# Values of the windowed attention as whole-width products, the second of each pair on exchanged token blocks

## The chip, the cores and the metric

The kernel runs on one core of a Trainium2 chip. The metric is the device time of one launch in microseconds. The engines: PE (TensorE, matrix products, with weight loads shown as PEld), ACT (ScalarE), DVE (VectorE), POOL (GpSimd) and SP (SyncE, which here issues the DMAs). They run side by side, each its own instruction list in order, and wait for each other through semaphores.

## The reference, cut to what matters

The whole program is four blocks of cross attention and feed-forward on x of 16 x 256 tokens and 128 channels. The change touches one stage, the six layers of windowed self-attention with a feed-forward part (`_L0_ffn_ref`), which takes some 3540 us of the span:

```
x  = shift_tokens(x)                     # channels 64..127 from the token before
q, k, v = split(x @ Wqkv)                # 16 heads of 64
q = l2norm(q) * q_scale;  k = l2norm(k) * k_scale      # then rotary tables with a scale
out = softmax(mask(q @ k_two_windows.T * 8)) @ v_two_windows   # windows of 32 tokens: own and the one before
x = out @ Wo + x
x = ffn_layer(shift_tokens(x)) + x       # layer norm, W1, a * gelu(gate), W2
```

## The kernel before, in words

A layer's 4096 tokens are worked through in 8 passes of 512 tokens (two sequences); 6 layers make 48 passes. A pass has four tiles of 128 tokens, and each tile two groups g of 8 heads, that is four pairs of heads; tile and group together are a chunk. The matrix of V and the output matrix are folded into one, `w_vo`, beforehand, so that "values" are already of 128 output channels per head. For a chunk's group and head n of each pair, the values of a token are 4 x 128 = 512 numbers.

The engines' lists are written out by hand, in `body(p)` of each engine. One round r of a pass projects q and k of tile r (`project_k`, `project_q`), makes the values of tile r's first group and of tile r-1's second group, transposes the rotated q and k of tile r-1 (`turn_q`, `turn_k`), forms its scores, and transposes the probabilities of tile r-2 and mixes its values (`turn_prob`, `mix`). The feed-forward of earlier passes is spread between: `down_proj` and `turn_normed` stand in round 1, the three `gate_proj` in round 2, `up_proj` in rounds 3 and 0. The prediction calls rounds 0 to 3 the first to the fourth. The traces' times below begin with round 1 at 2409.68 us, round 2 at 2428.79, round 3 at 2446.74, round 0 at 2466.47; a pass repeats every 74.43 us.

Values (PE, L825 to L840). `mix` and its window scheme want the two halves of a tile (64 tokens each) side by side: of slot j of `vo`, partitions 64n to 64n+63 hold head n's values of token half j. So `values(t, g, j)` takes the 64 tokens of half j as weights and makes two products of 64 x 512, one for each head of the pairs, into the two partition halves of bank V. `values_a` is half j = 0, `values_b` half j = 1. Both use the one bank V: ACT copies it to `vo` in one instruction of 128 x 512 (`copy_values`, L1290), and PE waits for that copy before it writes the bank again. In PE's list, `values_a` and `values_b` of the second group have project_k, turn_q, turn_prob, project_q and turn_k as neighbours; those of the first group stand between `mix` and `scores`, which work in column strips of 32.

In the trace a float32 product is two records, so the 768 pairs of products at L830 are 3072 records, and one values step of the timeline shows "x4", a whole-width one "x2".

After the copies SP moves the values by 32 partitions to `vo_off` by DMA (`shift_values`, L677), for the windows that begin at odd multiples of 32; `mix` reads `vo` or `vo_off`. `copy_q` (ACT, L1299) brings q to SBUF before `turn_k` may overwrite bank T; `copy_k` (L1304) is already written as two instructions of 64 x 512, one per partition half. `square` (L1283) makes the squares of q and k, after which DVE rotates them (`rotate`, L1036). On POOL, `add_up` and `scale` finish the rotation; `add_up` of the second group is the last of a round, and POOL then waits for the norms.

Of the kernel before, what the change touches and what calls it, by code (L numbers as in the profile page):

```python
# [20 lines left out]
ACT = mybir.ActivationFunctionType  # L21
# [450 lines left out]
def shifted_layers(nc, x_all, ident, ident_bf, dram):  # L472
# [18 lines left out]
    with ExitStack() as ctx:  # L491
# [24 lines left out]
        xs_t = sb("xs_t", [128, 2, SEQ])  # L516
        squares = sb("squares", [128, 2, 2, 512])
# [42 lines left out]
        xs_made = [sem(f"xs_made{s}") for s in range(2)]  # L560
        fold_in, fold_done, fold_made, fold_out = sem("fold_in"), sem("fold_done"), sem("fold_made"), sem("fold_out")
# [48 lines left out]
        def _(sp):  # L610
# [66 lines left out]
            def shift_values(p, t, g):  # L677


                i = 2 * t + g  # L680
                at = 2 * (t % 2)
                sp.wait_ge(vb_copied, count(p, i))
                alone(sp)
                sp.wait_ge(mixed, count(p, i - 4))
                alone(sp)
                for n in range(2):
                    r = 64 * n
                    sp.dma_start(vo_off[r + 32:r + 64, g, at:at + 2, :], vo[r:r + 32, g, at:at + 2, :]).then_inc(vo_moved[g][t % 2], 16)
                    if t % 2:
                        sp.dma_start(vo_off[r:r + 32, g, 2:4, :], vo[r + 32:r + 64, g, 1:3, :]).then_inc(vo_moved[g][t % 2], 16)  # L690
                    else:
                        sp.dma_start(vo_off[r:r + 32, g, 1, :], vo[r + 32:r + 64, g, 0, :]).then_inc(vo_moved[g][t % 2], 16)
# [97 lines left out]
        def _(pe):  # L790
# [17 lines left out]

            def project_k(p, t, g):
# [15 lines left out]
            def values(t, g, j):  # L825


                x = chunk_x(t)[:, 64 * j:64 * j + 64]
                for n in range(2):
                    done = nc.tensor.matmul(bank[V][64 * n:64 * n + 64, :], x, w_vo[:, 4 * g:4 * g + 4, n, :], start=True, stop=True)  # L830
                return done

            def values_a(p, t, g):
                pe.wait_ge(w_vo_in[g], (p + t // PASS_TILES) * 16 + 16)
                pe.wait_ge(vb_copied, count(p, 2 * t + g - 1))
                values(t, g, 0).then_inc(va_done, 1)

            def values_b(p, t, g):
                pe.wait_ge(va_copied, count(p, 2 * t + g))
                values(t, g, 1).then_inc(vb_done, 1)  # L840
# [14 lines left out]
            def scores(p, t, g):  # L855
# [4 lines left out]
                for b in range(4):  # L860
                    for w in range(4):
# [4 lines left out]
                            k_t[:, :, 4 * g + b, at:at + 64],  # L866
# [337 lines left out]
        def _(pool):  # L1204
# [10 lines left out]

            def add_up(p, t, g):
# [20 lines left out]
            def body(p):  # L1237
                for r in range(PASS_TILES):
# [16 lines left out]
                    if on(r):  # L1255
                        add_up(p, r, 1)

# [3 lines left out]
        def _(act):  # L1261
# [28 lines left out]
            def copy_values(p, t, g, j):  # L1290
# [6 lines left out]
                nc.scalar.activation(vo[:, g, 2 * (t % 2) + j, :], flat(V), ACT.Copy).then_inc((va_copied, vb_copied)[j], 1)  # L1297
# [2191 lines left out]
```

## Time and profile before

| | before |
|---|---|
| median of 3 runs | 4854.38 us (4852.14 to 4854.57) |
| profiled execution, its own time | 4843.04 us |
| its span in the profile | 4841.2 us |
| PE busy, share of the span | 4259.6 us, 88% |
| DVE, ACT, POOL busy | 3564.2, 2826.2, 2217.0 us |
| mean granted clock | 0.935 |

Shares of busy time are averages over stages. In the long stretch of the layers each engine's work repeats with every pass, so a timeline of one pass shows all of it. A timeline row is: start in us, duration in us, engine, line, operation, what it writes and reads, how many instructions were merged, and in brackets the idle time before it and what ended that.

### The profile page before, as it was taken

The page shows a single profiled execution, that of the slowest core. Times are in us where ns is not written, and L with a number is a line of the kernel's source. Part 1 is how long each engine was busy: PE and PEld are TensorE (multiplying, and loading weights), DVE is VectorE, ACT ScalarE, POOL GpSimd, SP SyncE. Part 2 cuts the span into 40 slices and gives each one's busy share as a digit, 9 for nine tenths or more (in the row PEclk, how much of TensorE's full clock was granted, in tenths as well). Part 3 has the DMA queues.
Part 4 walks back from the last instruction along what each step waited for, and adds up shares of the span by engine and source line. Part 5 has one row for each costly group of instructions (what it writes and reads, how often), then busy time and mean ns, then how long its engine had stood idle before and what let it go on. Part 6 is the DMA issues. An engine that isn't in the chain of part 4 may idle for free. (4 is left out here: it accounts for less than half of the span.)

```text
span 4841.2 us, 113325 instructions
## 1 busy us (share of the span) xinstructions
PE 4259.6 (88%) x40622; PEld 2404.1 (50%) x40622; DVE 3564.2 (74%) x8488; ACT 2826.2 (58%) x5112; POOL 2217.0 (46%) x1393
## 2 busy tenths in 40 slices
PE   8969999999999999999999999999999964746646
PEld 5645555554555555545555555555555532535534
DVE  6878888887888888878888888788888847456430
ACT  3436666666666666666666666666666635645301
POOL 0006555555555555555555555555555510030015
PEclk9989999999999999999999999999999975868558
DMA  1012222322223222232222322223222210000202
GB/s 40 1 59 65 59 58 55 78 59 56 58 53 77 64 54 59 54 77 62 54 56 60 74 63 54 58 56 74 61 60 54 58 25 1 12 1 6 77 11 30
DMA packets 187686, 245.93 MB, mean 51 GB/s; under 512 B 88661, under 2 KB 129367, under 8 KB 187224
## 3 DMA queue, kind: packets, MB, share of 16 engines
q1 hardware_dynamic: 181912, 239.95, 21.3%
q0 software_dynamic: 5632, 4.33, 0.7%
q8 instruction: 60, 0.98, 0.1%
q14 instruction: 82, 0.67, 0.0%
HBM read 41.13 MB, written 14.30 MB: 11 GB/s over the span
## 5 line engine op out<-in xcount | busy, mean ns | idle before, releaser
L1229 POOL TENSOR_TENSOR f_rot_a<-f_rot_a,f_norm 128x1024 f32<-128x1024 f32 x384 | 731.1, 1904 | 1106.7 <-DVE f_norm L1072 1074.2
L1221 POOL TENSOR_TENSOR f_rot_a<-f_rot_a,f_rot_b 128x1024 f32<-128x1024 f32 x384 | 907.4, 2363 | 353.8 <-issue 298.3
L830 PE MATMUL f_bank<-f_w_vo,f_xs_t 128*64 128x512 f32 x3072 | 828.5, 617 | 9.7 <-ACT f_vo L1297 9.7
L1297 ACT ACTIVATE f_vo<-f_bank 128x512 f32<-128x512 f32 x768 | 457.7, 596 | 579.0 <-PE f_bank L830 572.6
L1288 ACT ACTIVATE f_squares<-f_bank 128x512 f32<-128x512 f32 x768 | 459.1, 598 | 330.2 <-PE f_bank L817 244.5
L1051 DVE TENSOR_TENSOR f_rot_a<-f_bank,f_rot 128x512 f32<-128x512 f32 x768 | 526.8, 686 | 86.3 <-POOL f_rot_a L1221 41.6
L1054 DVE TENSOR_TENSOR f_rot_b<-f_bank,f_rot 128x512 f32<-128x512 f32 x768 | 514.2, 670 | 0.0
L1100 DVE TENSOR_REDUCE f_stat<-f_score 128x8 f32<-128x512 f32 x384 | 262.0, 682 | 280.5 <-ACT f_score L1314 280.5
L1058 DVE TENSOR_REDUCE f_sums<-f_squares 128x16 f32<-128x1024 f32 x384 | 465.1, 1211 | 3.3
L1309 ACT ACTIVATE f_k_t<-f_bank 64x512 f32<-64x512 f32 x768 | 450.4, 586 | 4.8 <-PE f_bank L852 0.3
L817 PE MATMUL f_bank<-f_w_qk,f_xs_t 128*128 128x512 f32 x768 | 431.7, 644 | 7.4 <-ACT f_xs_t L1279 5.9
L887 PEld LDWEIGHTS f_bank<-f_vo_off,f_prob_t 128*32 128x32 f32 x6144 | 309.6, 109 | 242.4 <-issue 242.4
L1235 POOL TENSOR_TENSOR f_prob<-f_score,f_stat 128x512 f32<-128x512 f32 x384 | 401.0, 1044 | 47.0 <-DVE f_stat L1104 47.0
L863 PE MATMUL f_bank<-f_k_t,f_q_t 128*32 128x128 f32 x12288 | 415.0, 276 | 0.0
L887 PE MATMUL f_bank<-f_vo,f_prob_t 128*32 128x128 f32 x6144 | 412.3, 276 | 0.0
L887 PE MATMUL f_bank<-f_vo_off,f_prob_t 128*32 128x128 f32 x6144 | 412.3, 276 | 0.0
L823 PE MATMUL f_bank<-f_w_qk,f_xs_t 128*128 128x512 f32 x768 | 394.0, 595 | 0.4 <-DVE f_rot_b L1054 0.4
L1302 ACT ACTIVATE f_q_t<-f_bank 128x512 f32<-128x512 f32 x384 | 229.0, 596 | 276.6 <-PE f_bank L846 276.6
L863 PEld LDWEIGHTS f_bank<-f_k_t,f_q_t 128*32 128x32 f32 x12288 | 312.0, 109 | 155.4 <-issue 155.4
L1092 DVE TENSOR_REDUCE f_stat<-f_bank 128x8 f32<-128x512 f32 x384 | 262.6, 684 | 132.4 <-PE f_bank L863 131.6
L887 PEld LDWEIGHTS f_bank<-f_vo,f_prob_t 128*32 128x32 f32 x6144 | 309.6, 109 | 0.0
L852 PE MATMUL f_bank<-ident,f_rot_a 128*128 128x128 f32 x1536 | 233.3, 274 | 53.4 <-ACT f_q_t L1302 53.3
(447 smaller groups left out, 7249.8 us busy)
## 6 DMA issues: line engine op xcount, KB each, us to landing
f_vo_off<-f_vo SPq DMA_DIRECT2D x1152, 128.0 KB, 2.3
f_vo_off<-f_vo SPq DMA_DIRECT2D x384, 64.0 KB, 2.0
f_w_qk<-in_Wqk SPq DMA_DIRECT2D x12, 512.0 KB, 5.5
f_vo_dram<-f_vo_pair SPq DMA_DIRECT2D x48, 128.0 KB, 1.8
f_x_shifted<-s_all SPq DMA_DIRECT2D x48, 128.0 KB
f_x_shifted<-s_all SPq DMA_DIRECT2D x48, 127.0 KB
f_w_vo<-f_vo_dram SPq DMA_DIRECT2D x10, 512.0 KB, 4.0
e_w<-in_e_W SPq DMA_DIRECT2D x2, 2048.0 KB
```

The lines of the kernel that those rows point to most:

```text
L817: nc.tensor.matmul(flat(K), chunk_x(t), w_qk[:, 1, 512 * g:512 * g + 512], start=True, stop=True).then_inc(k_done, 1)
L830: done = nc.tensor.matmul(bank[V][64 * n:64 * n + 64, :], x, w_vo[:, 4 * g:4 * g + 4, n, :], start=True, stop=True)
L863: done = nc.tensor.matmul(bank[S][32 * w:32 * w + 32, 128 * b:128 * b + 128], q_t[:, g, 128 * b + 32 * w:128 * b + 32 * w + 32], k_t[:, :, ...
L887: done = nc.tensor.matmul(bank[Y][32 * w:32 * w + 32, 0:128], prob_t[:, g, 128 * b + 32 * w:128 * b + 32 * w + 32], source[:, g, 2 * (t % ...
L1051: nc.vector.tensor_tensor(rot_a[:, slot, n, :].rearrange("p (h d) -> p h d", h=GROUP), source, c_tab, ALU.mult)
L1054: nc.vector.tensor_tensor(rot_b[:, g, n, :].rearrange("p (h s d) -> p h s d", h=GROUP, s=2), swapped, s_tab, ALU.mult).then_inc((q_rotated ...
L1058: nc.vector.tensor_reduce(sums[:, g, :], squares[:, g, :, :].rearrange("p n (h d) -> p (n h) d", h=GROUP), AX_X, ALU.add).then_inc(lengths, 1)
L1221: nc.gpsimd.tensor_tensor(rot_a[:, slot, :, :], rot_a[:, slot, :, :], rot_b[:, g, :, :], ALU.add).then_inc(rot_summed, 1)
L1229: nc.gpsimd.tensor_tensor(heads, heads, over(norm[:, 16 * g:16 * g + 16], [128, 16, HEAD_DIM]), ALU.mult).then_inc(qk_normed, 1)
L1288: nc.scalar.activation(squares[:, g, n, :], flat((Q, K)[n]), ACT.Square).then_inc((q_squared, k_squared)[n], 1)
L1297: nc.scalar.activation(vo[:, g, 2 * (t % 2) + j, :], flat(V), ACT.Copy).then_inc((va_copied, vb_copied)[j], 1)
L1309: done = nc.scalar.activation(k_t[r:r + 64, n, 4 * g:4 * g + 4, at:at + 128], flat(T)[r:r + 64, :].rearrange("p (b n) -> p b n", b=4), ACT ...
```

## The change

The two products of a values step are no longer split by head of the pair on 64 tokens, but one product of all 128 tokens for one head: `values(p, t, g, j)` makes head j of every pair. For j = 1 its weights are the tokens with their two blocks of 64 exchanged (`xs_swap`, made by POOL in `swap_x`, twice a pass, in rounds 1 and 3 behind `add_up`), so that the partition halves fall to the slots that `mix` wants; in slot 1 the heads then stand exchanged. Each bank is copied by two ACT instructions of 64 x 512, whose halves go to different slots. The loads to `vo_off` take the exchanged partitions, and the scores read k of the second window half with its heads exchanged.

```
@@ -514,6 +514,7 @@
         band = sb("band", [128, 2, 512], BF16)
         xw = sb("xw", [128, 2, SEQ])
         xs_t = sb("xs_t", [128, 2, SEQ])
+        xs_swap = sb("xs_swap", [128, 2, 2, 2, 64])
         squares = sb("squares", [128, 2, 2, 512])
         rot_a = sb("rot_a", [128, 4, 2, 512])
         rot_b = sb("rot_b", [128, 2, 2, 512])
@@ -558,6 +559,7 @@
         x_taken = [sem(f"x_taken{s}") for s in range(2)]
         x_turned = [sem(f"x_turned{s}") for s in range(2)]
         xs_made = [sem(f"xs_made{s}") for s in range(2)]
+        xs_swapped = [sem(f"xs_swapped{s}") for s in range(2)]
         fold_in, fold_done, fold_made, fold_out = sem("fold_in"), sem("fold_done"), sem("fold_made"), sem("fold_out")
         vo_moved = [[sem(f"vo_moved{g}{h}") for h in range(2)] for g in range(2)]
 
@@ -687,9 +689,9 @@
                     r = 64 * n
                     sp.dma_start(vo_off[r + 32:r + 64, g, at:at + 2, :], vo[r:r + 32, g, at:at + 2, :]).then_inc(vo_moved[g][t % 2], 16)
                     if t % 2:
-                        sp.dma_start(vo_off[r:r + 32, g, 2:4, :], vo[r + 32:r + 64, g, 1:3, :]).then_inc(vo_moved[g][t % 2], 16)
+                        sp.dma_start(vo_off[r:r + 32, g, 2:4, :], vo[96 - r:128 - r, g, 1:3, :]).then_inc(vo_moved[g][t % 2], 16)
                     else:
-                        sp.dma_start(vo_off[r:r + 32, g, 1, :], vo[r + 32:r + 64, g, 0, :]).then_inc(vo_moved[g][t % 2], 16)
+                        sp.dma_start(vo_off[r:r + 32, g, 1, :], vo[96 - r:128 - r, g, 0, :]).then_inc(vo_moved[g][t % 2], 16)
 
             def shift_x(p, q):
 
@@ -806,6 +808,10 @@
                 t = t % PASS_TILES
                 return xs_t[:, t // 2, 128 * (t % 2):128 * (t % 2) + 128]
 
+            def swapped_x(t):
+                t = t % PASS_TILES
+                return xs_swap[:, t // 2, t % 2, :, :].rearrange("p b n -> p (b n)")
+
             def project_k(p, t, g):
                 i = 2 * t + g
                 pe.wait_ge(w_qk_in[g], p * 16 + 16)
@@ -822,22 +828,22 @@
                 pe.wait_ge(q_rotated, count(p, i - 1))
                 nc.tensor.matmul(flat(Q), chunk_x(t), w_qk[:, 0, 512 * g:512 * g + 512], start=True, stop=True).then_inc(q_done, 1)
 
-            def values(t, g, j):
-
-
-                x = chunk_x(t)[:, 64 * j:64 * j + 64]
-                for n in range(2):
-                    done = nc.tensor.matmul(bank[V][64 * n:64 * n + 64, :], x, w_vo[:, 4 * g:4 * g + 4, n, :], start=True, stop=True)
-                return done
+            def values(p, t, g, j):
+
+                x = chunk_x(t)
+                if j:
+                    pe.wait_ge(xs_swapped[(t % PASS_TILES) // 2], p + t // PASS_TILES + 1)
+                    x = swapped_x(t)
+                return nc.tensor.matmul(flat(V), x, w_vo[:, 4 * g:4 * g + 4, j, :], start=True, stop=True)
 
             def values_a(p, t, g):
                 pe.wait_ge(w_vo_in[g], (p + t // PASS_TILES) * 16 + 16)
                 pe.wait_ge(vb_copied, count(p, 2 * t + g - 1))
-                values(t, g, 0).then_inc(va_done, 1)
+                values(p, t, g, 0).then_inc(va_done, 1)
 
             def values_b(p, t, g):
                 pe.wait_ge(va_copied, count(p, 2 * t + g))
-                values(t, g, 1).then_inc(vb_done, 1)
+                values(p, t, g, 1).then_inc(vb_done, 1)
 
             def turn_q(p, t, g):
                 pe.wait_ge(qk_normed, count(p, 2 * t + g))
@@ -863,7 +869,7 @@
                         done = nc.tensor.matmul(
                             bank[S][32 * w:32 * w + 32, 128 * b:128 * b + 128],
                             q_t[:, g, 128 * b + 32 * w:128 * b + 32 * w + 32],
-                            k_t[:, :, 4 * g + b, at:at + 64],
+                            k_t[:, ::(-1 if w >= 2 else 1), 4 * g + b, at:at + 64],
                             start=False, stop=True, skip_group_check=True)
                 done.then_inc(scores_done, 1)
 
@@ -1213,6 +1219,15 @@
 
             nc.gpsimd.tensor_copy(xw[:, 0, :], x_all[:, 0:SEQ]).then_inc(x_taken[0], 1)
 
+            def swap_x(s, p):
+                pool.wait_ge(xs_made[s], p * 2 + 2)
+                if not isinstance(p, int) or p > 0:
+                    pool.wait_ge(vb_done, count(p, 4 * s - 5))
+                alone(pool)
+                nc.gpsimd.tensor_copy(xs_swap[:, s, :, :, :], xs_t[:, s, :].rearrange("p (t b n) -> p t b n", t=2, b=2)[:, :, ::-1, :]).then_inc(xs_swapped[s], 1)
+
+            swap_x(0, 0)
+
             def add_up(p, t, g):
                 slot = 2 * (t % 2) + g
                 pool.wait_ge(k_rotated, count(p, 2 * t + g))
@@ -1254,6 +1269,10 @@
                         weigh(p, r - 1, 0)
                     if on(r):
                         add_up(p, r, 1)
+                    if r == 1 and has(p, 0):
+                        swap_x(1, p)
+                    if r == 3 and has(p, -1):
+                        swap_x(0, p + 1)
 
             stream(pool, body)
 
@@ -1294,7 +1313,10 @@
 
                     act.wait_ge(mixed, count(p, i - 4))
                     act.wait_ge(vo_moved[g][(t - 1) % 2], moved(p, t - 1))
-                nc.scalar.activation(vo[:, g, 2 * (t % 2) + j, :], flat(V), ACT.Copy).then_inc((va_copied, vb_copied)[j], 1)
+                for half in range(2):
+                    r = 64 * half
+                    done = nc.scalar.activation(vo[r:r + 64, g, 2 * (t % 2) + (half ^ j), :], flat(V)[r:r + 64, :], ACT.Copy)
+                done.then_inc((va_copied, vb_copied)[j], 1)
 
             def copy_q(p, t, g):
                 act.wait_ge(q_turned, count(p, 2 * t + g))
```

In the list of ACT, rounds 2 and 3 of a pass inside the loop, `f_vo` are the values' copies, `f_gate` the gate's copies and gelu, `f_xs_t` the shifted tokens, `f_score` the exponential, `f_q_t` the copy of q. Before:

```order
L1297 ACTIVATE f_vo<-f_bank 128x512
L1334 REGISTER_ALU
L1335 ACTIVATE f_gate<-f_bank,f_cols 85x512
L1340 ACT_TABLE_LOAD
L1340 ACTIVATE f_gate<-f_gate 128x512 x2
L1340 ACTIVATE f_gate<-f_gate 85x512
L1297 ACTIVATE f_vo<-f_bank 128x512
L1285 REGISTER_ALU
L1288 ACTIVATE f_squares<-f_bank 128x512
```

and with the change:

```order
L1318 ACTIVATE f_vo<-f_bank 64x512 x2
L1356 REGISTER_ALU
L1357 ACTIVATE f_gate<-f_bank,f_cols 85x512
L1362 ACT_TABLE_LOAD
L1362 ACTIVATE f_gate<-f_gate 128x512 x2
L1362 ACTIVATE f_gate<-f_gate 85x512
L1318 ACTIVATE f_vo<-f_bank 64x512 x2
L1304 REGISTER_ALU
L1307 ACTIVATE f_squares<-f_bank 128x512
```

Nothing changes place; each copy of the values is two rows in one.

In the list of POOL, rounds 1 and 2 of a pass inside the loop, `f_rot_a<-f_rot_a,f_rot_b` is `add_up`, `f_rot_a<-f_rot_a,f_norm` is `scale`, `f_prob` the weighing. With the change:

```order
L1236 TENSOR_TENSOR f_rot_a<-f_rot_a,f_rot_b 128x1024
L1223 ISA
L1227 COPY f_xs_swap<-f_xs_t 128x256
L1244 TENSOR_TENSOR f_rot_a<-f_rot_a,f_norm 128x1024
L1250 TENSOR_TENSOR f_prob<-f_score,f_stat 128x512
```

The exchange stands between the last `add_up` of round 1 and the first `scale` of round 2, which followed each other before.

## Rows read from the trace of the kernel before

**Rows 1.** Stretch of the layers: engines' busy time (instructions), granted clock, DMA share, GB/s

```profile
core 0: us, PE busy (x) PEld busy (x) DVE busy (x) ACT busy (x) POOL busy (x), PEclk, DMA share, GB/s
700.00:3800.00 3100.00, 2984.03 (x31535) 1595.06 (x31534) 2518.20 (x5368) 2033.08 (x3586) 1785.75 (x1083) 1.00 0.27 61
```

**Rows 2.** PE's timeline in round 1, around the second group's products

```profile
2414.42 0.66 PE L846 MATMUL f_bank<-ident,f_rot_a 128*128 128x128 f32 x4
2414.91 0.60 PE L874 MATMUL f_bank<-ident,f_prob 128*128 128x128 f32 x4
2415.35 1.02 PE L823 MATMUL f_bank<-f_w_qk,f_xs_t 128*128 128x512 f32 x2
2416.21 0.60 PE L852 MATMUL f_bank<-ident,f_rot_a 128*128 128x128 f32 x4
2416.74 1.08 PE L830 MATMUL f_bank<-f_w_vo,f_xs_t 128*64 128x512 f32 x4
2417.75 1.12 PE L817 MATMUL f_bank<-f_w_qk,f_xs_t 128*128 128x512 f32 x2
2418.71 0.38 PE L859 MATMUL f_bank<-f_band,ident_bf 128*128 128x512 bf16 x1
```

**Rows 3.** PE's timeline in round 0, the first group's products and scores

```profile
2405.31 1.08 PE L830 MATMUL f_bank<-f_w_vo,f_xs_t 128*64 128x512 f32 x4
2406.32 0.39 PE L859 MATMUL f_bank<-f_band,ident_bf 128*128 128x512 bf16 x1
...
2407.66 1.08 PE L830 MATMUL f_bank<-f_w_vo,f_xs_t 128*64 128x512 f32 x4
```

**Rows 4.** The costliest groups: busy us, mean ns of one, idle before it

```profile
L1309 ACT ACTIVATE f_k_t<-f_bank 64x512 f32<-64x512 f32 x768 | 450.4, 586 | 4.8 <-PE f_bank L852 0.3
```

**Rows 5.** ACT's timeline in rounds 0 and 1

```profile
2406.44 0.60 ACT L1297 ACTIVATE f_vo<-f_bank 128x512 f32<-128x512 f32 x1 [0.30 <-PE f_bank L830]
...
2415.11 0.60 ACT L1302 ACTIVATE f_q_t<-f_bank 128x512 f32<-128x512 f32 x1
...
2416.90 1.18 ACT L1309 ACTIVATE f_k_t<-f_bank 64x512 f32<-64x512 f32 x2
2418.11 0.60 ACT L1297 ACTIVATE f_vo<-f_bank 128x512 f32<-128x512 f32 x1
2418.91 0.60 ACT L1288 ACTIVATE f_squares<-f_bank 128x512 f32<-128x512 f32 x1 [0.20 <-PE f_bank L817]
```

**Rows 6.** ACT's timeline from the end of round 2 into round 3

```profile
2443.50 0.60 ACT L1297 ACTIVATE f_vo<-f_bank 128x512 f32<-128x512 f32 x1 [0.94 <-PE f_bank L830]
2443.99 0.68 ACT L1335 ACTIVATE f_gate<-f_bank,f_cols 85x512 f32<-85x512 f32 x1
...
2447.56 0.57 ACT L1297 ACTIVATE f_vo<-f_bank 128x512 f32<-128x512 f32 x1
...
2451.25 0.60 ACT L1297 ACTIVATE f_vo<-f_bank 128x512 f32<-128x512 f32 x1
2451.74 0.59 ACT L1302 ACTIVATE f_q_t<-f_bank 128x512 f32<-128x512 f32 x1
```

**Rows 7.** PE's timeline in round 3, the product and turn_k that wait for ACT

```profile
2448.28 1.08 PE L830 MATMUL f_bank<-f_w_vo,f_xs_t 128*64 128x512 f32 x4 [0.20 <-ACT f_vo L1297]
...
2452.39 0.66 PE L852 MATMUL f_bank<-ident,f_rot_a 128*128 128x128 f32 x4 [1.15 <-ACT f_q_t L1302]
```

**Rows 8.** DVE's timeline in round 1, the rotation of k of the second group

```profile
2419.54 0.69 DVE L1051 TENSOR_TENSOR f_rot_a<-f_bank,f_rot 128x512 f32<-128x512 f32 x1
```

**Rows 9.** PE's timeline in round 1, the transposes of the normed tokens

```profile
2422.83 0.66 PE L909 MATMUL f_bank<-ident,f_f_n 128*128 128x128 f32 x4 [0.41 <-DVE s_all L1146]
```

**Rows 10.** POOL's timeline, the first scaling behind round 1's last add_up

```profile
2426.20 1.90 POOL L1229 TENSOR_TENSOR f_rot_a<-f_rot_a,f_norm 128x1024 f32<-128x1024 f32 x1 [5.37 <-DVE f_norm L1072]
```

**Rows 11.** Engines' busy time in two stretches, columns as in rows 1

```profile
2446.00:2456.00 10.00, 8.65 (x63) 3.86 (x51) 7.07 (x16) 9.48 (x17) 7.33 (x5) 1.00 0.20 44
64.90:71.70 6.80, 6.18 (x20) 4.42 (x21) 4.84 (x10) 1.60 (x3) 0.00 (x0) 0.50 0.00 0
```

**Rows 12.** PE's timeline in the cross attention before the layers

```profile
63.36 0.33 PE L215 MATMUL x_bank<-ident,x_xn 128*128 128x128 f32 x1 [2.42 <-DVE x_xn L347]
```

More of the change, by code:

```diff
@@ L560, in shifted_layers @@
         xs_made = [sem(f"xs_made{s}") for s in range(2)]
+        xs_swapped = [sem(f"xs_swapped{s}") for s in range(2)]
         fold_in, fold_done, fold_made, fold_out = sem("fold_in"), sem("fold_done"), sem("fold_made"), sem("fold_out")
@@ L807, in chunk_x, with swapped_x @@
                 return xs_t[:, t // 2, 128 * (t % 2):128 * (t % 2) + 128]
+            def swapped_x(t):
+                t = t % PASS_TILES
+                return xs_swap[:, t // 2, t % 2, :, :].rearrange("p b n -> p (b n)")
             def project_k(p, t, g):
@@ L823, in project_q, with values @@
                 nc.tensor.matmul(flat(Q), chunk_x(t), w_qk[:, 0, 512 * g:512 * g + 512], start=True, stop=True).then_inc(q_done, 1)
[L825 to L831, printed above, removed]
+            def values(p, t, g, j):
+                x = chunk_x(t)
+                if j:
+                    pe.wait_ge(xs_swapped[(t % PASS_TILES) // 2], p + t // PASS_TILES + 1)
+                    x = swapped_x(t)
+                return nc.tensor.matmul(flat(V), x, w_vo[:, 4 * g:4 * g + 4, j, :], start=True, stop=True)
             def values_a(p, t, g):
@@ L1214, in _, with swap_x @@
             nc.gpsimd.tensor_copy(xw[:, 0, :], x_all[:, 0:SEQ]).then_inc(x_taken[0], 1)
+            def swap_x(s, p):
+                pool.wait_ge(xs_made[s], p * 2 + 2)
+                if not isinstance(p, int) or p > 0:
+                    pool.wait_ge(vb_done, count(p, 4 * s - 5))
+                alone(pool)
+                nc.gpsimd.tensor_copy(xs_swap[:, s, :, :, :], xs_t[:, s, :].rearrange("p (t b n) -> p t b n", t=2, b=2)[:, :, ::-1, :]).then_inc(xs_swapped[s], 1)
+            swap_x(0, 0)
             def add_up(p, t, g):
@@ L1256, in body @@
                         add_up(p, r, 1)
+                    if r == 1 and has(p, 0):
+                        swap_x(1, p)
+                    if r == 3 and has(p, -1):
+                        swap_x(0, p + 1)
             stream(pool, body)
@@ L1296, in copy_values @@
                     act.wait_ge(vo_moved[g][(t - 1) % 2], moved(p, t - 1))
-                nc.scalar.activation(vo[:, g, 2 * (t % 2) + j, :], flat(V), ACT.Copy).then_inc((va_copied, vb_copied)[j], 1)
+                for half in range(2):
+                    r = 64 * half
+                    done = nc.scalar.activation(vo[r:r + 64, g, 2 * (t % 2) + (half ^ j), :], flat(V)[r:r + 64, :], ACT.Copy)
+                done.then_inc((va_copied, vb_copied)[j], 1)
             def copy_q(p, t, g):
```

11 lines of the change are left out of this document (6 added, 5 removed).

## The prediction

> **What bounds the kernel now.** I read the busy time of the steady stretch first, then the timeline of TensorE (PE) over the rounds, then that of ScalarE (ACT) wherever PE was idle, then VectorE (DVE). Over 3100 us of the six layers PE is busy for 2984 us at full clock, ACT for 2033, DVE for 2518 [rows 1]. So PE looks like the bound, and less PE work should be time gained. The timelines qualify that: PE waits at fixed places in every pass, and two of them matter here. In the fourth round ACT runs from 2443.50 to copy_q at 2451.74 without a pause, three value copies among its work [rows 6], and PE stands idle for it, 0.20 us before a product and 1.15 us before turn_k [rows 7]. In the second round PE waits 0.41 us for DVE before it transposes the normed tokens [rows 9]. At such places PE's speed is worth nothing, and ACT's or DVE's is worth everything.
>
> There are 48 passes (6 layers of 8); 46 of them hold the gelu work of the pass two before, and I count those 46.
>
> **PE: what is saved.** Each product is now four records in two column halves, and takes 1.01 us to the next step's start (2416.74 to 2417.75). The whole-width product of the same size, project_q, takes 0.86 (2415.35 to 2416.21). Around the narrow product the neighbours are dearer as well: turn_k, 0.53 before one (2416.21 to 2416.74) against 0.44 of an equal block of four transposes (2414.91 to 2415.35); project_k, 0.96 behind one against 0.86; turn_q, 0.49 behind one against 0.44 [rows 2]. So entering or leaving a narrow mode costs 0.05 to 0.10. For the second head group the products stand among whole-width steps, so both crossings vanish: values_a saves 0.09 + 0.15 + 0.05 = 0.29 us, values_b 0.09 + 0.15 + 0.10 = 0.34. For the first group the neighbours are the 32-wide scores and mix: the crossings stay. There values_a costs 0.96 (as project_k behind a narrow step), a gain of 0.05, and values_b, narrow work on both sides, some 0.86 + 0.10 + 0.10 = 1.06, a loss of 0.05. Together 0.63 us a round, 2.5 us a pass, **116 us** over 46 passes if PE alone counted.
>
> **ACT: what is added.** Each copy of 128 x 512 becomes two of 64 x 512. Half the partitions is not half the time: the copies of k, already 64 x 512, take 586 ns each [rows 4], against 0.60 us of a whole copy [rows 5]. In a queue without idle time a whole copy costs only 0.49, since the next instruction starts before it ends (2443.50 to 2443.99 [rows 6]). The two halves of k, which work on partitions 0 to 63 and 64 to 127, take 1.18 us together and the next copy starts 1.21 after the first (2416.90 to 2418.11 [rows 5]): there is no overlap. So a value copy costs **0.72 us more where ACT is the chain, 0.58 where it waited for PE before**. The bounds: nothing (if halves took half), and 0.72; I take the row of k, which has the same shape, source and partition halves.
>
> The Trainium skill, page "ScalarE: Activation LUTs", section "What ACT_TABLE_LOAD costs", gives 186 ns plus 0.833 ns per element and an overlap of about 93 ns between instructions back to back. By that rule the second half would add about 0.52 us and the fourth round below some 0.6 us less a pass. The trace agrees on the 0.60 and on the overlap of whole copies, not on that of halves [rows 5, 6].
>
> **Round by round** (times of a product's start as zero, a wait's end costs PE about 0.06, from copy_q's end at 2452.33 to turn_k at 2452.39 [rows 6, 7]):
>
> Any round, turn_k of the first group. It needs copy_q, which ACT does behind the copy of values_a. PE would be there after 0.86 + 0.44 + 0.44 + 0.86 = 2.60 us. ACT gets there at 1.02 (the product's end) + 0.05 + 1.18 + 0.03 + 0.60 + 0.05 = 2.93. Today turn_k comes 0.50 after copy_q's end (2415.11 + 0.60, then 2416.21 [rows 2, 5]). The 0.33 of new wait eats the 0.29 gained. Net 0; values_b's 0.34 behind it remains.
>
> Any round, first group. Today values_a starts at 2405.31, its copy runs from 2406.44 to 2407.04, and values_b starts at 2407.66 [rows 3, 5]: 0.62 us of slack. Then: product's end 1.12, copies from 1.17 to 2.35, values_b at 2.40; PE alone would be there at 0.96 + 1.34 = 2.30. A new wait of 0.10, and 2.40 stands against today's 2.35; with values_b's own 0.05 the round loses **0.10**.
>
> Second round (with the down projection). ACT: copy_q at 2415.60 by the sum above, then three steps of 0.49 to the copies of k at 2417.07, values_b's copies at 2418.28, the square of k at 2419.49 instead of 2418.91 [rows 5]: 0.58 late. DVE's rotation of k starts on that square, at 2419.54 today [rows 8], and DVE works on without a pause from there to the residual that PE awaits at 2422.83; so the normed tokens are turned 0.58 later [rows 9] where PE's gain would have made them earlier. With the first group's 0.10: **+0.68**.
>
> Fourth round. The ACT chain holds three value copies, 2443.50, 2447.56 and 2451.25 [rows 6], each step 0.49 growing to 1.21: turn_k comes 3 x 0.72 = **2.16 us later**. Behind it PE gains 0.34 and the first group loses 0.10: +1.92.
>
> First and third round: -0.34 + 0.10 = -0.24 each.
>
> A pass: -0.24 + 0.68 - 0.24 + 1.92 = +2.12 us; 46 passes, **+98 us**.
>
> Free: the exchange of blocks on GpSimd, two copies of 128 x 256 a pass. No row has that copy; it is bounded by nothing and by the 1.90 of a rotated tile's scaling, and sits where GpSimd idles for 5.37 us [rows 10]. Were that cover gone, the scaling behind it would be that much later. The exchanged loads of SP keep their number and size; k read with its halves exchanged keeps its columns (unknown price, taken as 0). The new wait of values_b for the exchange is met a round or more ahead. SP's moves of the values come 0.6 us later, far ahead of the mix that wants them two rounds on.
>
> **The clock.** In the fourth round PE's idle stretch before turn_k grows from 1.15 us by 0.72 (the copy between) and 0.2 to 0.3 (its own faster steps) to about 2.2, and the 0.20 before the product to over 1 us. Today's stretch of these rounds is granted 1.00, that is 2.4 GHz [rows 11]. Elsewhere in this trace an idle stretch of 2.42 us [rows 12] was followed by 6.80 us at 0.50, 1.2 GHz [rows 11]. At half clock a PE-bound stretch of that length loses 3.4 us; part would lie beside ACT's chain, so I take half, 1.7 us, in three passes of four: 1.7 x 0.75 x 46 = 59 us, an estimate between 0 (no fall) and 3.4 x 46 = 156.
>
> **The sum.** The profiled execution took 4843 us: 4843 + 98 + 59 = 5000. The median of the runs, 4854, is 11 above it: **5011 us**.
>
> **Rivals.**
> The clock holds. PE was idle 1.15 us in each pass without a fall, and the new stretch is only twice that. Then 4843 + 98 + 11 = 4952. Chance 0.25.
> The halves overlap. Whole copies do, by 0.1, on the same queue [rows 6]. Then a copy costs 2 x 0.49, 0.49 more instead of 0.72: the fourth round 3 x 0.49 - 0.34 + 0.05 = 1.18, the second about 0.2, the others -0.4 each, 0.6 a pass, 28 us; with the shorter stall the clock holds: 4882. Against it speaks k's pair, 1.21 [rows 5]. Chance 0.10. It is what the Trainium skill's page on ScalarE would give.
> PE is the bound, and the copies vanish in ACT's idle third [rows 1]. It decides at a half copy's price: at 0.3 us or less the chain of the fourth round does not grow, the waits stay as they are, and most of the 116 us comes: 4843 - 116 + 11 = 4738, faster than before. Against it stand 586 ns for half the partitions [rows 4]. Chance 0.05.
> The wide product is no quicker than its two halves, since these run side by side today. Then the 0.34 a round is lost too, 63 us: 5074. Against it speaks project_q's 0.86 [rows 2]. Chance 0.03.
>
> **How the numbers follow.** My forecast has the remaining 0.57. The range reaches from the clock's rival with some 0.6 us a pass less (4952 - 27 = 4925) to falls that cost nearly all of 3.4 us in every pass (4843 + 98 + 156 + 11 = 5108, cut to 5095); outside lie the overlap, the faster rival and the tails, under 0.2. Faster by over 0.2% (about 10 us, what a measurement of this kernel can tell from no change) needs the PE rival or more than the overlap: 0.06. Within 0.2%: 0.02. Slower: 0.92.
>
> **What would show it.** ACT's copies at 64 x 512, twice as many, near 0.59 each; product records halved in number, spacing 0.86 for the second group; PE's wait for copy_q at some 2.2 us in every pass, and small ones in the other rounds; the wait for the residual near 1.3; granted clock under 1 in the steady stretch, with falls behind the fourth round's stall. I am wrong if the pair of halves costs under 0.9, if the passes come out under 74.4 us each, or if the clock stays at 1.00 (then 4952).

## The result and the profile after

The changed kernel takes 5038.43 us (median of 4 runs, 5036.84 to 5042.46), the kernel before 4853.26 (4 runs on the same chip): a ratio of 1.0385, 95% interval 1.0372 to 1.0398. It is slower by 3.9%. The forecast was 5011, its range 4925 to 5095. The profiled execution took 5037.6 us with a span of 5035.8, 194.6 more than before. One of the nine runs of the kernel before that stand beside e11 below took 7153 us (granted clock 0.59), and the ratio there leaves it out.

The busy time of each engine, the first part of the page:

```profile
PE 4196.7 (83%) x38701; PEld 2528.9 (50%) x39086; DVE 3560.6 (71%) x8488; ACT 3292.2 (65%) x5880; POOL 2243.3 (45%) x1490
```

The costliest groups, columns as in [rows 4]: the copies, the products and turn_k. Before:

```profile
L830 PE MATMUL f_bank<-f_w_vo,f_xs_t 128*64 128x512 f32 x3072 | 828.5, 617 | 9.7 <-ACT f_vo L1297 9.7
L1297 ACT ACTIVATE f_vo<-f_bank 128x512 f32<-128x512 f32 x768 | 457.7, 596 | 579.0 <-PE f_bank L830 572.6
...
L852 PE MATMUL f_bank<-ident,f_rot_a 128*128 128x128 f32 x1536 | 233.3, 274 | 53.4 <-ACT f_q_t L1302 53.3
```

And after:

```profile
L1318 ACT ACTIVATE f_vo<-f_bank 64x512 f32<-64x512 f32 x1536 | 907.0, 591 | 517.9 <-PE f_bank L837 503.4
...
L837 PE MATMUL f_bank<-f_w_vo,f_xs_swap 128*128 128x512 f32 x768 | 436.9, 652 | 20.7 <-ACT f_vo L1318 2.6
L837 PE MATMUL f_bank<-f_w_vo,f_xs_t 128*128 128x512 f32 x768 | 415.7, 623 | 67.9 <-ACT f_vo L1318 67.9
L858 PE MATMUL f_bank<-ident,f_rot_a 128*128 128x128 f32 x1536 | 246.8, 284 | 142.3 <-ACT f_q_t L1324 142.2
```

PE has 1536 product records where it had 3072, and is busy for 83% of the span instead of 88%. ACT's copies of the values take 907.0 us, where the whole ones took 457.7. PE's wait for copy_q before turn_k (L858) has grown from 53.3 us to 142.2.

**Where the time went.** The rows of project_k's first product mark the rounds. PE's timeline, the start of the second, third and fourth round and of the next pass, with the places that the prediction spoke of between them:

```profile
2515.69 1.12 PE L823 MATMUL f_bank<-f_w_qk,f_xs_t 128*128 128x512 f32 x2
...
2519.33 1.02 PE L837 MATMUL f_bank<-f_w_vo,f_xs_t 128*128 128x512 f32 x2
2520.19 0.60 PE L852 MATMUL f_bank<-ident,f_rot_a 128*128 128x128 f32 x4
...
2522.26 0.66 PE L858 MATMUL f_bank<-ident,f_rot_a 128*128 128x128 f32 x4 [0.17 <-ACT f_q_t L1324]
2522.76 1.02 PE L837 MATMUL f_bank<-f_w_vo,f_xs_swap 128*128 128x512 f32 x2
2523.62 1.02 PE L823 MATMUL f_bank<-f_w_qk,f_xs_t 128*128 128x512 f32 x2
...
2529.39 0.66 PE L915 MATMUL f_bank<-ident,f_f_n 128*128 128x128 f32 x4 [1.20 <-DVE s_all L1152]
...
2535.54 1.12 PE L823 MATMUL f_bank<-f_w_qk,f_xs_t 128*128 128x512 f32 x2
...
2537.36 1.02 PE L837 MATMUL f_bank<-f_w_vo,f_xs_t 128*128 128x512 f32 x2
...
2540.53 0.66 PE L858 MATMUL f_bank<-ident,f_rot_a 128*128 128x128 f32 x4 [0.41 <-ACT f_q_t L1324]
...
2553.58 1.12 PE L823 MATMUL f_bank<-f_w_qk,f_xs_t 128*128 128x512 f32 x2
...
2556.38 1.10 PE L837 MATMUL f_bank<-f_w_vo,f_xs_t 128*128 128x512 f32 x2 [1.45 <-ACT f_vo L1318]
...
2561.35 1.12 PE L858 MATMUL f_bank<-ident,f_rot_a 128*128 128x128 f32 x4 [2.14 <-ACT f_q_t L1324]
...
2576.88 1.10 PE L823 MATMUL f_bank<-f_w_qk,f_xs_t 128*128 128x512 f32 x2
```

The values' products stand 0.86 us apart from the next step (2519.33 to 2520.19, 2522.76 to 2523.62), as forecast from project_q. But the fourth round, 2553.58 to some 2576.9, takes 23.3 us instead of 19.74. PE stands idle 1.45 us before its product and 2.14 before turn_k, where it was 0.20 and 1.15 [rows 7]; in the second round it waits 1.20 for the residual instead of 0.41 [rows 9].

ACT's timeline in the second round, in the third, and from the end of the third into the fourth (answering to [rows 5, 6]):

```profile
2524.28 1.19 ACT L1318 ACTIVATE f_vo<-f_bank 64x512 f32<-64x512 f32 x2
2525.50 0.60 ACT L1307 ACTIVATE f_squares<-f_bank 128x512 f32<-128x512 f32 x1
...
2538.15 0.62 ACT L1336 ACTIVATE f_score<-f_score 128x512 f32<-128x512 f32 x1
2538.67 1.18 ACT L1318 ACTIVATE f_vo<-f_bank 64x512 f32<-64x512 f32 x2
2539.88 0.60 ACT L1324 ACTIVATE f_q_t<-f_bank 128x512 f32<-128x512 f32 x1
...
2550.27 1.19 ACT L1318 ACTIVATE f_vo<-f_bank 64x512 f32<-64x512 f32 x2 [0.98 <-PE f_bank L837]
2551.49 0.68 ACT L1357 ACTIVATE f_gate<-f_bank,f_cols 85x512 f32<-85x512 f32 x1
...
2555.05 1.18 ACT L1318 ACTIVATE f_vo<-f_bank 64x512 f32<-64x512 f32 x2
...
2559.48 1.19 ACT L1318 ACTIVATE f_vo<-f_bank 64x512 f32<-64x512 f32 x2
2560.70 0.60 ACT L1324 ACTIVATE f_q_t<-f_bank 128x512 f32<-128x512 f32 x1
```

Each pair of halves holds the queue for 1.21 to 1.22 us (2538.67 to 2539.88, 2559.48 to 2560.70). From the first copy of the fourth round's chain to copy_q it was 8.24 us (2443.50 to 2451.74); now it is 10.43 (2550.27 to 2560.70). That is 2.19 more, three times 0.73.

The granted clock, with the engines' busy time (columns as in [rows 1]), over the steady stretch, then over 7 us that end within the stall before the fourth round's turn_k, and behind the stall:

```profile
700.00:3800.00 3100.00, 2784.69 (x28459) 1618.97 (x28779) 2392.53 (x5106) 2315.87 (x4042) 1718.63 (x1110) 0.98 0.26 58
...
2554.00:2561.00 7.00, 3.75 (x16) 1.78 (x14) 2.52 (x9) 6.85 (x13) 4.25 (x2) 1.00 0.28 62
2561.30:2564.60 3.30, 3.25 (x7) 1.92 (x8) 2.63 (x5) 2.55 (x5) 1.67 (x2) 0.50 0.00 0
```

PE is busy for 3.75 of these 7 us, ACT for 6.85. Then comes a stretch of 3.4 us at 0.50 (1.2 GHz). The profile has 36 such stretches in the layers, all in the 46 passes with gelu work, one a pass. A pass with one lasts 78.64 us and one without 76.94, so one costs 1.70.

The falls are not strewn at random. Twelve or eleven passes in a row have one, then three keep the clock. Within such a run the falls come 78.5 us apart, where the passes are 78.64 long, so each lies some 0.13 us earlier in its pass than the last. PE's stall before turn_k is 2.14 or 2.15 us in all of the 40 passes from the fifth on, with a fall or without.

The span difference of 194.6 us: (76.94 - 74.43) x 45 = 113; 36 x 1.70 = 61; the start and the first three passes, which are not yet of the steady length, 6; and some 15 behind the layers. That last part lies between 961 us (before) and 975 (after) in the kernels below, and is 975 too in one whose layers stayed as they were before but for the copies (e6), so it is not put down to the change.

### The profile page after: what moved, and what is told of

It reads as the page before. It is cut to its first block and busy times, and to the rows that moved or that the text cites. A ratio compares the mean times of both kernels' runs of the same rounds, so it can differ in the third digit from the quotient of the medians.

```text
span 5035.8 us, 111351 instructions
## 1 busy us (share of the span) xinstructions
PE 4196.7 (83%) x38701; PEld 2528.9 (50%) x39086; DVE 3560.6 (71%) x8488; ACT 3292.2 (65%) x5880; POOL 2243.3 (45%) x1490
## 5 line engine op out<-in xcount | busy, mean ns | idle before, releaser
L1318 ACT ACTIVATE f_vo<-f_bank 64x512 f32<-64x512 f32 x1536 | 907.0, 591 | 517.9 <-PE f_bank L837 503.4
L837 PE MATMUL f_bank<-f_w_vo,f_xs_t 128*128 128x512 f32 x768 | 415.7, 623 | 67.9 <-ACT f_vo L1318 67.9
L837 PE MATMUL f_bank<-f_w_vo,f_xs_swap 128*128 128x512 f32 x768 | 436.9, 652 | 20.7 <-ACT f_vo L1318 2.6
L858 PE MATMUL f_bank<-ident,f_rot_a 128*128 128x128 f32 x1536 | 246.8, 284 | 142.3 <-ACT f_q_t L1324 142.2
L858 PEld LDWEIGHTS f_bank<-ident,f_rot_a 128*128 128x128 f32 x1536 | 173.3, 143 | 301.3 <-ACT f_q_t L1324 301.3
```

What stands on the lines that cost most here:

```text
L837: return nc.tensor.matmul(flat(V), x, w_vo[:, 4 * g:4 * g + 4, j, :], start=True, stop=True)
L1318: done = nc.scalar.activation(vo[r:r + 64, g, 2 * (t % 2) + (half ^ j), :], flat(V)[r:r + 64, :], ACT.Copy)
```

## The experiments

All were run beside the kernel before. Each ratio is to the runs beside it. A round's length is the distance between project_k's first products (median of 40 passes, falls included); "falls" are the stretches at 1.2 GHz in the layers of the profiled execution.

| kernel | median us | ratio to before (95%) | rounds 1 / 2 / 3 / 4 | pass | falls |
|---|---|---|---|---|---|
| before | 4853.26 | 1 | 17.63 / 19.12 / 17.95 / 19.74 | 74.43 | 0 |
| the change | 5038.43 | 1.0385 (1.0372 to 1.0398) | 17.36 / 19.85 / 18.04 / 23.38 | 78.63 | 36 |
| e1 whole copies | 4760.27 | 0.9819 (0.9804 to 0.9834) | 16.91 / 18.81 / 17.29 / 19.45 | 72.45 | 0 |
| e2 halves only | 5043.4 | 1.0406 (1.0390 to 1.0422) | 17.93 / 19.93 / 18.31 / 21.99 | 78.16 | 11 |
| e3 filler | 4972.95 | 1.0255 (1.0239 to 1.0271) | 17.32 / 19.85 / 18.04 / 21.74 | 76.95 | 0 |
| e4 no exchange | 5036.57 | 1.0390 (1.0375 to 1.0404) | 17.36 / 19.85 / 18.04 / 23.38 | 78.64 | 40 |
| e5 chain whole | 4870.48 | 1.0037 (1.0023 to 1.0051) | 17.36 / 19.85 / 17.91 / 19.61 | 74.74 | 0 |
| e6 column halves | 4860.04 | 1.0017 (1.0007 to 1.0027) | 17.66 / 19.11 / 17.95 / 19.88 | 74.60 | 0 |
| e7 square first | 4998.75 | 1.0306 (1.0288 to 1.0323) | 17.36 / 19.26 / 18.04 / 23.38 | 78.05 | 34 |
| e8 halves on DVE | 4882.6 | 1.0069 (1.0052 to 1.0086) | 17.37 / 19.26 / 17.91 / 20.58 | 75.09 | 0 |
| e9 the same, early | 5070.85 | 1.0450 (1.0435 to 1.0464) | 17.25 / 19.69 / 22.47 / 19.33 | 78.86 | 47 |
| e10 moves first | 4852.25 | 1.0010 (1.0001 to 1.0019) | 17.25 / 19.69 / 17.58 / 19.87 | 74.38 | 0 |
| e11 order by round | 4833.9 | 0.9961 (0.9947 to 0.9975) | 17.21 / 19.27 / 17.58 / 19.87 | 73.96 | 0 |

### The two parts of the change, each alone

e1 is the changed kernel with one copy per bank:

```
-                for half in range(2):
-                    r = 64 * half
-                    done = nc.scalar.activation(vo[r:r + 64, g, 2 * (t % 2) + (half ^ j), :], flat(V)[r:r + 64, :], ACT.Copy)
-                done.then_inc((va_copied, vb_copied)[j], 1)
+                nc.scalar.activation(vo[:, g, 2 * (t % 2) + j, :], flat(V), ACT.Copy).then_inc((va_copied, vb_copied)[j], 1)
```

> The changed kernel with each bank of values copied in one instruction of 128 x 512; the second half of each copy so lands in the wrong slot, and the values are not those of the reference. Theory (the whole-width products gain, the split copies lose more): without the split, a pass loses 0.63 us in the first and third round each, almost nothing in the second (DVE is the bound there), 0.34 in the fourth behind ACT's chain: -1.6 us a pass, 46 passes, about 4778, no fall of the clock. Rival (the products or the exchange are what costs): at or above 4853.

Its pass is 1.98 us shorter than before, its time 1.8% less. So the whole-width products do gain, by more than the 1.6 us that were expected; 0.31 of it comes in the second round, which was expected to give almost nothing. The slower result lies in the copies. ACT's group of copies is what it was:

```profile
L1316 ACT ACTIVATE f_vo<-f_bank 128x512 f32<-128x512 f32 x768 | 457.7, 596 | 575.8 <-PE f_bank L837 569.2
```

e2 is the kernel before with its copy written as two of 64 x 512, into the same slot:

```
-                nc.scalar.activation(vo[:, g, 2 * (t % 2) + j, :], flat(V), ACT.Copy).then_inc((va_copied, vb_copied)[j], 1)
+                for half in range(2):
+                    r = 64 * half
+                    done = nc.scalar.activation(vo[r:r + 64, g, 2 * (t % 2) + j, :], flat(V)[r:r + 64, :], ACT.Copy)
+                done.then_inc((va_copied, vb_copied)[j], 1)
```

> The kernel before with its narrow products and its layout, and each value copy in two instructions of 64 x 512. Theory (ACT's added time alone makes the loss): first and third round +0.2 each, second +0.8, fourth +2.2, some +3.4 us a pass or 156 us, and the clock falls in about three passes of four (59 us): about 5067, more than the changed kernel. Rival (products and exchange make the loss): near 4853.

The split alone makes the kernel 4.1% slower, as much as the whole change. Its rounds grow by 0.30, 0.81, 0.36 and 2.25 us. The falls were fewer than expected, 11, and so the time is under the expected 5067. The stall before turn_k is a little shorter here than the 2.14 us of the change:

```profile
2408.45 0.66 PE L852 MATMUL f_bank<-ident,f_rot_a 128*128 128x128 f32 x4 [2.01 <-ACT f_q_t L1305]
```

### What the stall does to the clock

e3 puts seven bf16 products into the stall of the fourth round, into the scores' bank that turn_k doesn't need:

```
+                    if r == 3 and has(p, 2) and on(r - 1):
+                        pe.wait_ge(shifted, count(p, 2 * (r - 1) - 1))
+                        for _ in range(7):
+                            nc.tensor.matmul(flat(S), ident_bf[:, :], band[:, 0, :], start=True, stop=True)
```

> The changed kernel with seven products of 128 x 512 in bf16 into the free bank of the scores, in PE's wait before turn_k of the fourth round; nobody reads them. Theory (the stall, not the stage, brings the clock down): all passes 76.9 us, no fall, 34 x 1.70 = 58 us less than the changed kernel, about 4980. Rival (the falls come from something else): falls remain, 5038 or a little more.

PE's timeline at that place:

```profile
2444.36 1.67 PE L979 MATMUL f_bank<-f_band,ident_bf 128*128 128x512 bf16 x7
2446.67 0.66 PE L858 MATMUL f_bank<-ident,f_rot_a 128*128 128x128 f32 x4 [0.64 <-ACT f_q_t L1328]
```

The busy time and clock of its steady stretch:

```profile
700.00:3800.00 3100.00, 2886.38 (x29536) 1651.63 (x29533) 2432.07 (x5199) 2355.08 (x4110) 1749.46 (x1127) 1.00 0.26 59
```

The stall is filled but for 0.64 us, turn_k starts no earlier, and the falls are gone: every pass takes 76.95 us and the kernel is 65 us quicker, though PE does more. So it is the stall before turn_k that brings the falls; the wait of 1.46 us before the product of that round is still there. They cost what the passes of the change showed: 36 x 1.70 = 61 of the 64 us between the two spans (the expectation had counted 34 falls).

### The exchange of blocks

e4 leaves the exchange out (`swap_x`, its wait in `values`, and the reversed heads in the scores).

> The changed kernel without the exchange: the second product takes the tokens in their order, GpSimd makes no copies, the scores read k in its order. The values are then not those of the reference. Theory: the exchange is hidden, 5038 within 8 us. Rival (the copies delay GpSimd's scaling, or the reversed reading of k costs PE): at least 0.3 us a pass less, 5024 or below.

All four rounds stay to the hundredth, and the time is the same: the exchange costs nothing. In the changed kernel POOL's timeline shows where it stands:

```profile
2536.15 2.35 POOL L1236 TENSOR_TENSOR f_rot_a<-f_rot_a,f_rot_b 128x1024 f32<-128x1024 f32 x1 [0.49 <-issue]
2538.44 0.40 POOL L1227 COPY f_xs_swap<-f_xs_t 128x256 f32<-128x256 f32 x1
2538.80 1.90 POOL L1244 TENSOR_TENSOR f_rot_a<-f_rot_a,f_norm 128x1024 f32<-128x1024 f32 x1
```

It takes 0.40 us, and the scaling follows at once: it sits between two busy pieces, not in an idle stretch, and makes that scaling some 0.4 us later.

### Which copies cost, and why two halves do

e5 writes whole the three copies that stand in the chain of the fourth round (third tile, all but the last):

```
+                if t % PASS_TILES == 2 and not (g and j):
+                    nc.scalar.activation(vo[:, g, 2 * (t % 2) + j, :], flat(V), ACT.Copy).then_inc((va_copied, vb_copied)[j], 1)
+                    return
```

> The changed kernel with the three value copies of ACT's chain into the fourth round (both of the third tile's first group, the first of its second group) as whole copies; their second halves land in wrong slots, and the values are not those of the reference. Theory (each split copy in that chain makes turn_k 0.72 us later, and the stall so grown brings the clock down): 2.16 us less a pass than the 76.94 of a pass without a fall, that is 74.8, and no falls: about 4870. Rival (the loss is spread over all copies alike): three of sixteen copies, less than 40 us off the changed kernel.

As expected: the fourth round is back at 19.61, under the 19.74 before, and the clock holds. 3 of 16 copies carried 168 of the 185 us, the falls included.

e6 is the kernel before with each copy in two halves by columns (128 x 256) instead of partitions:

```
+                for half in range(2):
+                    c = 256 * half
+                    done = nc.scalar.activation(vo[:, g, 2 * (t % 2) + j, c:c + 256], flat(V)[:, c:c + 256], ACT.Copy)
+                done.then_inc((va_copied, vb_copied)[j], 1)
```

> The kernel before with each value copy in two instructions of 128 x 256, by columns instead of partitions. Theory (a half of the columns is cheaper, 0.39 us, and instructions that begin on the same partition overlap): a pair costs 0.58 in a queue, 0.09 more than a whole copy; about 0.5 us a pass, 4872. Rival (two instructions on one bank never overlap): a pair costs 0.78 to 0.8, 0.3 more; the fourth round alone 0.9 later, 4900 or above.

ACT's timeline of the last copy before copy_q:

```profile
2456.08 0.66 ACT L1299 ACTIVATE f_vo<-f_bank 128x256 f32<-128x256 f32 x2
2456.62 0.60 ACT L1305 ACTIVATE f_q_t<-f_bank 128x512 f32<-128x512 f32 x1
```

The group of copies:

```profile
L1299 ACT ACTIVATE f_vo<-f_bank 128x256 f32<-128x256 f32 x1536 | 503.8, 380 | 572.4 <-PE f_bank L830 566.1
```

The pair takes 0.54 us of the queue, against 0.49 for a whole copy and 1.21 for the halves by partitions. So it is not the second instruction that costs. Two things do: a half by partitions has all 512 columns to run through (591 ns against 380), and the two halves do not overlap, as these do (2 x 0.38 = 0.76, done in 0.66). The Trainium skill, page "ScalarE: Activation LUTs", section "What ACT_TABLE_LOAD costs", has instructions back to back overlap by about 93 ns: the trace agrees for these column halves, not for the pair of halves by partitions.

In these traces the step to the other partitions stops the overlap, not the half width. In e8 below ACT copies only the half on partitions 0 to 63 of the three copies in the chain. ACT's timeline there, the third of them and copy_q:

```profile
2474.89 0.59 ACT L1341 ACTIVATE f_vo<-f_bank 64x512 f32<-64x512 f32 x1
2475.39 0.58 ACT L1347 ACTIVATE f_q_t<-f_bank 128x512 f32<-128x512 f32 x1
```

That single half overlaps copy_q by 0.09 us, as a whole copy does. In the change's trace the second half of a pair, on partitions 64 to 127, starts 0.01 us behind the end of the first, and where ACT has no wait the next instruction starts 0.02 us behind the second.

### Can the copies be moved out of the way?

e7 swaps two steps in ACT's list, `square(p, r, 1, 1)` ahead of `copy_values(p, r - 1, 1, 1)`, in the changed kernel.

> The changed kernel with ACT's square of k for the second group ahead of the copy of the second group's second product, in every round. Theory (in the second round DVE waits for that square, which the longer copy delays by 0.58 us): the second round falls from 19.85 to 19.2 or 19.4, the others stay within 0.1; about 0.5 us a pass, 5012, falls as before. Rival (DVE's own queue sets that round): 19.8, 5036.

Only the second round changes, 19.85 to 19.26. So the delay of that round came through the square of k, as the prediction had it. The time is 13 us under the expected 5012: 7 of them lie behind the layers and 3 in two falls fewer.

e8 adds to e7 that DVE takes the second half of the three copies in the chain:

```
+            def halve(p, t, g, j):
...
+                nc.vector.tensor_copy(vo[64:128, g, 2 * (t % 2) + (1 ^ j), :], flat(V)[64:128, :]).then_inc(v_halved, 1)
...
-                for half in range(2):
+                for half in range(1 if t % PASS_TILES == 2 and not (g and j) else 2):
```

> A version that should keep the gain: the last one, and for the three copies of ACT's chain the second half is copied by DVE, which idles there, so that ACT's chain is as long as before the change. Theory: rounds of 17.3, 19.3, 18.0 and 19.4 or 19.5, some 74.1 us a pass, no falls, 4835 within 20, at or under the kernel before. Rival (DVE's added work delays its own chain): 75 us a pass or more, above 4870.

It missed: 4882.6, with a fourth round of 20.58. DVE's timeline shows the reason:

```profile
2471.76 0.70 DVE L1169 COPY f_vo<-f_bank 64x512 f32<-64x512 f32 x1
2474.37 0.87 DVE L1129 BATCH_NORM_STATS2 f_f_stats<-f_x_shifted 128x6 f32<-128x128 f32 x4 [1.91 <-DMA f_x_shifted<-s_all]
2475.28 0.69 DVE L1169 COPY f_vo<-f_bank 64x512 f32<-64x512 f32 x1
```

The third half copy stands behind the statistics, and these wait for a DMA.

e9 puts that half copy ahead of the statistics, issues the DMA (`shift_x`) ahead of the round's moves of the values on SP, and puts copy_q ahead of the copy of values_a of the second group on ACT.

> The version before this one with three moves: DVE makes its third half copy ahead of the statistics that wait for a DMA, SP issues the loads of the shifted tokens ahead of the moves of the third round, and ACT copies q ahead of the values. Theory (the fourth round was long because DVE came late to that half, behind the DMA): the fourth round falls from 20.6 to 19.5 to 19.9, the others by 0 to 0.2, some 73.8 to 74.4 us a pass, 4820 to 4850, level with or just under the kernel before. Rival (DVE has no room for the halves in that stretch): fourth round above 20.3, above 4865.

The fourth round came down to 19.33, but the third rose to 22.47, with 47 falls. SP's timeline at that place, the last of the shift's three issues and the fourth of the moves behind it:

```profile
2407.97 6.46 SPq L709 DMA_DIRECT2D f_x_shifted<-s_all  x1
...
2416.56 0.59 SPq L696 DMA_DIRECT2D f_vo_off<-f_vo  x1
```

ACT's timeline there, the copy of values_a of the next tile's first group:

```profile
2419.03 0.59 ACT L1343 ACTIVATE f_vo<-f_bank 64x512 f32<-64x512 f32 x1 [4.77 <-DMA f_vo_off<-f_vo]
```

PE's, the product that comes behind:

```profile
2419.86 2.04 PE L841 MATMUL f_bank<-f_w_vo,f_xs_swap 128*128 128x512 f32 x2 [3.43 <-DVE f_vo L1169]
```

The last issue of the shift holds SP for 6.46 us, as in the other runs, the moves of the tile before come behind it, and ACT's next copy, which overwrites a slot that the first four of them read, waits 4.77 us until they have landed. PE waits 3.43 us in turn, and at this wait the clock falls, in each of the 46 passes.

e10 puts SP's order back and keeps the rest.

> e9_dve_halves_early with one part undone: SP issues the shifted tokens behind round 2's moves of the values again, as before. The order on ACT (copy_q ahead of the copy of values_a of the second group) and on DVE (third half copy ahead of the statistics) stay. Theory: the third round's 22.5 us there came from the moves issued late alone. Then the rounds are 17.25, 19.7, 17.9 and 19.4 us, the pass 74.2 to 74.4, the clock holds, and the time is level with the kernel before: 4835 to 4860. Rival: the third round rose since copy_q stands ahead of the values' copy. Then it stays at 22 us or more, the pass at 78 us, and the time over 5030. Third possibility: DVE's half copy ahead of the statistics holds up later work of DVE: the fourth round over 20 us, 4880 or more.

The third round is 17.58 and the kernel level with the one before. The moves were the cause. The fourth round stayed at 19.87, above the 19.4 expected: there PE waits for the half copy on DVE, 0.84 us against the 0.20 of [rows 7].

```profile
2452.37 1.12 PE L841 MATMUL f_bank<-f_w_vo,f_xs_t 128*128 128x512 f32 x2 [0.84 <-DVE f_vo L1169]
```

e11 differs from e10 in one round: in the second, copy_q stands behind the copy again.

```
+                        if r == 1:
+                            copy_values(p, r - 1, 1, 0)
                         copy_q(p, r - 1, 0)
-                        copy_values(p, r - 1, 1, 0)
+                        if r != 1:
+                            copy_values(p, r - 1, 1, 0)
```

> e10_moves_first with ACT's copy_q ahead of the copy of values_a of the second group in every round but the second, where it stands behind that copy again, as before. Theory: each round's length follows ACT's queue ahead of what PE and DVE wait for, so the second round returns from 19.69 to the 19.26 us of e7 and e8 and the others stay: 17.25, 19.26, 17.6 and 19.9 us, a pass of 74.0 us against 74.43 before, no falls of the clock, and 4820 to 4840, under the kernel before by 0.2 to 0.5%. Rival: what the second round gives back, a later one loses, since a chain over several rounds on POOL and DVE sets the pass: then the pass stays at 74.3 to 74.4 us and the time level with the kernel before, 4845 to 4855.

The theory holds: 4833.9 us, under the kernel before by 0.4% (interval 0.25% to 0.53%). It is the one version that leaves nothing out and beats both, the kernel before (4846 to 4855 us beside it) and the change.

## Why the prediction was right, step by step

| term, us a pass | predicted | measured |
|---|---|---|
| first round | -0.24 | -0.27 |
| second round | +0.68 | +0.73 |
| third round | -0.24 | +0.09 |
| fourth round, at full clock | +1.92 | +1.94 |
| a fall of the clock | 1.7, in 3 passes of 4 | 1.70, in 36 of 46 |

**PE's gain** was 0.86 per product as read from project_q. e1, whose copies are whole, bears it out: -1.98 a pass, where the sum for PE alone was 2.5; part of that goes into longer waits, 1.28 us before turn_k of the fourth round (1.15 before) and 0.76 for the residual in the second (0.41 before).

**ACT's price** was the term that decided. The row of k's halves [rows 4, 5] gave 1.21 for a pair, and the values' pairs take 1.21 to 1.22. The rival of overlapping halves, 4882, is out for these halves; e6 shows halves that do overlap. The rival in which PE is the bound is out as well, since PE's share fell and the waits grew.

**The first round** came out right partly by luck. PE's row of up_proj there, before:

```profile
2468.12 1.09 PE L929 MATMUL f_bank<-f_f_nt,f_w 128*85 128x512 f32 x2 [0.55 <-DVE f_gate L1139]
```

and with the change:

```profile
2578.30 1.09 PE L935 MATMUL f_bank<-f_f_nt,f_w 128*85 128x512 f32 x2 [0.32 <-DVE f_gate L1145]
```

This wait for DVE became 0.23 us shorter, which no term of the sum has (why DVE is sooner is not shown), while turn_k and what stands behind it came out some 0.20 dearer than the sum.

**The second round** went as said: the square of k came behind both halves (2525.50), DVE's rotation behind it, and PE waits 1.20 us for the residual, against the 1.3 forecast. e7 undid just that link.

DVE's row of that rotation, which answers to [rows 8]:

```profile
2526.13 0.69 DVE L1057 TENSOR_TENSOR f_rot_a<-f_bank,f_rot 128x512 f32<-128x512 f32 x1 [0.49 <-ACT f_squares L1307]
```

**The third round** is the term that was mis-sized. The sum for "any round, turn_k of the first group" let the copy of values_a start 0.05 us behind the product's end. In this round it doesn't: the product ends at 2538.38 (2537.36 + 1.02) and the copy starts at 2538.67, behind the gate's copy and the exponential. So turn_k starts 3.17 us behind the product (2537.36 to 2540.53) where the sum had 2.93 and the second round has 2.93 (2519.33 to 2522.26): 0.24 of the missing 0.33 us is this. In e10 and e11 copy_q passes that copy in this round, which takes 17.58 there; e8, which differs from e10 in that and in the place of DVE's half, has 17.91.

**The sum.** The profiled execution came out 38 us above the 5000 of the sum: 15 in the rounds (113 against 98, nearly all of it the third round's), 6 in the start and the first passes, 15 behind the layers and 2 on the clock. The sum had no term for the first passes or for what lies behind the layers. The median lies 27 above the forecast, since it was only 1 above the profiled execution this time, not 11.

**The fourth round** holds to 0.02 us, by its own mechanism: 2.19 us of ACT's chain against the 2.16 forecast, and e5 takes it away with the three copies named. At turn_k it is 2.12 (5.65 us behind the round's start before, 7.77 now), 0.04 under the forecast, and PE's gain behind turn_k is 0.18 instead of 0.24; the two nearly cancel.

**The clock** was the guess with the widest bounds, 0 to 156 us, and its middle came out right, 61 us against 59, by luck. The prediction took a stretch of 6.8 us, as in [rows 11], and half of its 3.4 us of loss; the falls are 3.4 us long and cost all of their 1.70. Three passes of four was a guess without a row behind it. That the stall brings the falls is right, and shown by e3. Why some passes keep the clock is open: the length of the stall does not decide it, since it is the same in all of them.

**"Free"** was right in price and wrong in its cover. The 5.37 us of idle time [rows 10] stand ahead of the scaling of the first group, not behind the round's last add_up, as the heading there has it; the exchange stands behind that add_up, with hardly any idle time. e4 shows that the delay costs nothing; that turn_q needs the scaling's result only later is how the lists read, not measured. And "SP's moves come 0.6 us later, far ahead of the mix" looked at one reader only. The next copy into the slot waits for them too. In the change no wait for them shows; in e9 it cost 4.9 us in the third round and 4.5 a pass against e10, the falls included.

## What to carry to other kernels

On ACT an eviction's price went by its columns, not its partitions (591 ns for 64x512, 596 for 128x512, 380 for 128x256). Before a product is rearranged so that its result must be copied by partition halves, count those copies on the engine whose queue is the chain, at the price of the nearest row with that shape. One pass had 16 such copies, and the three in the chain of one round decided nearly everything. When a stall on PE grows, count the clock as a term of its own, and when a step on a DMA queue is moved, look for every reader and for the next writer of its source.

## What was not expected of the hardware

- Two copies of 128 x 256 take 0.54 us of ACT's queue, two of 64 x 512 on either half of the partitions take 1.21, for the same bytes. A single 64 x 512 on partitions 0 to 63 takes 0.50 (e8).
- PE's crossing between whole-width and 64-wide products costs 0.05 to 0.10 us each way in [rows 2], and with it gone the products came out at 0.86 to the next step. The Trainium skill, page "TensorEngine Tiling (Array Packing)", section "Key Properties", says that changing the tiling mode drains the engine; it gives no time, and the rows do.
- The clock fell behind stalls of 2.0 to 2.2 us in very different numbers of the 46 passes: 36, 40 and 33 at 2.14 to 2.15 us (the change, e4, e7), 11 at 2.01 (e2). It fell in all 46 at 3.3 us or more (e9), and in none where PE's longest stall was 1.5 us or less (before, e1, e3, e5, e6, e8, e10, e11).
- Work added to PE (1.67 us a pass in e3) made the kernel 65 us quicker.
